# A two-layer sequence model in one launch: from four window stages in turn to five time blocks interleaved beside the experts

## What is computed

```
h = layernorm(x) * (1 + ca) + sa            # layer 0
q, k = l2norm(silu(conv4(silu(h W + b)))),  v = silu(conv4(silu(h Wv + bv)));  a, b = sigmoid(h Wa + ba), sigmoid(h Wb + bb)
S_t = a S - a b (S k) k^T + b v k^T;  o_t = q S_t          # 16 heads of 8x8, gated delta rule over 256 steps
x += ga * (o Wo + bo)
h = layernorm(x) * (1 + cb) + sb
x += gb * (h + sum over the top 2 of 8 experts of gate * (silu(h We1 + be1) We2 + be2))   # hidden size 512
h = layernorm(x) * (1 + ca') + sa'          # layer 1
x += ga' * out_proj(ssd(conv4(in_proj(h))))   # decaying state, normalised by its own weights
h = layernorm(x) * (1 + cb') + sb'
x += gb' * (down(gelu(up(h))))              # butterfly factors, folded once into two dense matrices
```

## Time and profile before

| | us |
|---|---|
| median of 3 runs | 811.51 |
| lowest and highest | 810.26, 816.49 |
| profiled execution, whole time | 816.03 |
| profiled execution, span of the core | 814.2 |

### The profile page before, as it was taken

The page is one execution under the profiler, slowest core; times in us unless marked ns, Lnnn a source line. Parts: engine busy times, 40 slices in busy tenths (PEclk is TensorE's granted clock), DMA queues, the critical chain, the costliest instruction groups (busy, mean ns, idle before and its releaser), DMA issues.

```text
span 814.2 us, 5816 instructions
## 1 busy us (share of the span) xinstructions
PE 503.1 (62%) x1910; PEld 285.1 (35%) x1910; DVE 379.4 (47%) x684; ACT 288.6 (35%) x397; POOL 249.8 (31%) x248
## 2 busy tenths in 40 slices
PE   6545146726639972537699826366898626999424
PEld 3113135312326630212377402123575212567101
DVE  1142489332647726666466366662665360012250
ACT  3343023244214344515244235233441523442222
POOL 1346323255511136347011262662112301100202
PEclk9976668755959995567899955579799756999656
DMA  9405450003320000130500000505000000000000
GB/s 322 175 0 116 105 180 14 0 0 93 88 52 1 1 0 0 43 72 14 116 1 1 0 0 3 114 0 130 0 1 1 0 0 0 14 1 1 0 0 13
DMA packets 9437, 34.08 MB, mean 42 GB/s; under 512 B 2488, under 2 KB 2496, under 8 KB 8128
## 3 DMA queue, kind: packets, MB, share of 16 engines
q1 hardware_dynamic: 9408, 33.71, 15.3%
HBM read 30.56 MB, written 3.15 MB: 41 GB/s over the span
## 4 chain that ended last, share of the span: by engine, by line
PE 37%; DVE 20%; ACT 7%; DMA 4%; issue 3%; POOL 2%; SPq 1%; POOLq 0%; DVEq 0%; ACTq 0%
PE psS L550 12%; PE psF L540 12%; DMA wrep<-scratch_dram 3%; PE psM L506 3%; DVE XK L982 2%; DVE work L952 2%; DVE work L980 2%; PE psB L441 2%; SPq L411 1%; PE psF L632 1%; PE psA L439 1%; PE psF L584 1%; DVE acc L991 1%; PE psS L497 1%; PE psF L578 1%
## 5 line engine op out<-in xcount | busy, mean ns | idle before, releaser
L540 PE MATMUL psF<-h,we1s 128*128 128x512 f32 x256 | 127.2, 630 | 39.4 <-ACT hid L807 38.6
L550 PEld LDWEIGHTS psS<-we2s,hid 128*128 128x128 f32 x1024 | 120.9, 195 | 15.1 <-issue 15.1
L807 ACT ACTIVATE hid<-psF,col 128x512 f32<-128x512 f32 x128 | 87.3, 686 | 97.5 <-PE psF L540 97.4
L550 PE MATMUL psS<-we2s,hid 128*128 128x128 f32 x1024 | 120.6, 277 | 0.0
L1296 POOL TENSOR_TENSOR work<-H,work 128x512 f32<-128x512 f32 x32 | 41.8, 1306 | 219.6 <-DVE H L1027 219.6
L991 DVE SCALAR_TENSOR_TENSOR acc<-psS,gate,acc 128x128 f32<-128x128 f32 x128 | 35.9, 343 | 103.8 <-PE psS L550 103.8
L540 PEld LDWEIGHTS psF<-h,we1s 128*128 128x128 f32 x256 | 42.7, 195 | 103.4 <-ACT hid L807 85.3
L441 PE MATMUL psB<-sq,C 128*128 128x512 f32 x32 | 29.8, 1031 | 47.2 <-ACT sq L700 47.2
L758 ACT ACTIVATE A<-ag 128x512 f32<-128x512 f32 x32 | 19.7, 626 | 98.9 <-DVE H L1027 98.9
L1010 DVE TENSOR_TENSOR pbuf<-wrep,H 128x512 f32<-128x512 f32 x32 | 22.5, 704 | 59.1 <-DMA wrep<-scratch_dram 58.8
L439 PE MATMUL psA<-x,C 128*128 128x512 f32 x32 | 27.0, 939 | 29.5 <-POOL x L1335 9.1
(11 more groups left out here) (191 smaller groups left out, 847.5 us busy)
## 6 DMA issues: line engine op xcount, KB each, us to landing
krep<-scratch_dram SPq DMA_DIRECT2D x32, 256.0 KB, 5.8
wrep<-scratch_dram SPq DMA_DIRECT2D x32, 256.0 KB, 5.9
hid<-fold_mats_dram SPq DMA_DIRECT2D x22, 256.0 KB, 8.1
we1s<-we_dram SPq DMA_DIRECT2D x1, 2048.0 KB, 12.3
we2s<-we_dram SPq DMA_DIRECT2D x1, 2048.0 KB, 16.7
x<-xT_dram SPq DMA_DIRECT2D x4, 256.0 KB, 6.8
scratch_dram<-work SPq DMA_DIRECT2D x4, 256.0 KB, 2.0
scratch_dram<-XK SPq DMA_DIRECT2D x4, 256.0 KB, 2.0
```

Source lines behind the costliest of these rows:

```text
L540: mm(psF[n % 2][:, :], we1s[:, e, k * P:(k + 1) * P], h2[:, :], start=True, stop=True).then_inc(s_hid_mm, 1)
L550: last = mm(psS[n % 2][:, t * P:(t + 1) * P], hid[n % 2][:, k, t * P:(t + 1) * P], we2s[:, e, k, :], start=(k == 0), stop=(k == HT - 1))
L807: nc.scalar.activation(hid[(EXPERTS * w + e) % 2][:, k, :], psF[n % 2][:, :], ACT.Silu, bias=pc("be1", HT * e + k)).then_inc(s_hid_done, 1)
```

## The change

The time axis is cut into five blocks of 32, 32, 64, 64 and 64 steps (`TWS`) instead of four of 64. SSD and FFN keep blocks of 64 (`BW`): block v is complete after the expert block given by `finished`. The loop becomes six rounds r. In round r each engine's queue is written out by expert e and quarter q: PE issues `first(r, e, q)` and a quarter of `second(r, e - 1, q)`, ACT `hidden(r, e, q)`, and between them stand, at fixed slots (e, q), the front of block r + 2 (LayerNorm, projections, convolution, norms, key products), the scan, attention output and router of block r + 1, and SSD and FFN of the block that round r - 1 finished. The last expert's `second` and last two mixes of a round fall into the next round. Front products use the banks X0, X1 (the two halves of `psM`) from block 2 on; router and attention output use `psB`.

Other parts: DVE solves for keys and values in one operation with two right sides (`solve`, in place of `solve_keys` and `solve_values`). LayerNorm scale and shift are eight activations per tile on ACT (`modulate`), one per sequence, instead of two tensor operations on POOL. The first convolution tap is computed by ACT (`first_taps`). `hidden` asks for Silu's table set before each tile. Query products and attention output work on halves of 32 steps. `h2`, `ag`, `gate` and `acc` get two buffers, `hf` holds one block and a carried column, `c3`/`KK`/`u` share `zb`. In the prologue only blocks 0 and 1 get a front; folding lies between their steps, and SP issues four of the later fold loads, then the spreads of block 0, then the other fold loads.

The other slots, as (e, q):
- PE: SSD center (2,0), variance (2,1), `ssd_in` (3,1), `ssd_out` (5,0); FFN center (5,3), variance (6,0), `ffn_up` (7,1) and (7,2), `ffn_down` (7,3); front center (2,2), variance (2,3), `project` (3,2) to (4,0), `square_sums` (5,2), `key_products` (6,2) to (7,0); `attn_out` (4,2) and (6,1); router's LayerNorm (7,0) and (7,1), `router` (7,3).
- ACT: `ln_square`, then one slot later `ln_scale` and `modulate`: SSD (2,0) (2,1), front (2,2) (2,3), FFN (5,3) (6,0), router (7,0) (7,1); `ssd_in` (3,1), `ssd_exp` (4,0), `ssd_norm` (4,3); `projected` (3,3) to (4,1), `first_taps` (4,1), `convolved` (5,2), `norms` (5,3); `attn_branch` (4,3) and (6,2); `ffn_act` (7,2), `ffn_out` and `routed` (7,3).
- DVE, by e, after that step's mix and chunks: `ssd_halo` 1, SSD LayerNorm 2, `ssd_decay` 3, `ssd_norm` 4, `ssd_branch` 5; front LayerNorm 2, `convolve` 5, `couple` 6 and 7; FFN LayerNorm 6; router's LayerNorm 7.

```diff
-WINDOWS = 4
-TW = SEQ // WINDOWS
+TWS = [32, 32, 64, 64, 64]
+W = len(TWS)
+T0 = [sum(TWS[:w]) for w in range(W + 1)]
+HALF = 32
+BW = 64
...
@@ PE @@
+            for r in range(W + 1):
+                vs = finished(r - 1) if r > 0 else []
+                v = vs[0] if vs else None
+                n, o = r + 2, r + 1
+                for e in range(EXPERTS):
+                    for q in range(4):
+                        if r < W:
+                            first(r, e, q)
+                        if e > 0 and r < W:
+                            second(r, e - 1, q)
+                        elif e == 0 and 0 < r:
+                            second(r - 1, EXPERTS - 1, q)
+                        if (e, q) == (0, 0) and r < W:
+                            logits(r)
+                        if (e, q) == (1, 0) and r < W:
+                            gate_rows(r)
+                        if (e, q) == (1, 1) and r < W:
+                            router_bias(r)
+                        if (e, q) == (1, 2) and r > 0:
+                            experts_back(r - 1)
...
 # in the same way: ssd center (2,0), variance (2,1), ssd_in (3,1), ssd_out (5,0), ffn center (5,3), variance (6,0),
 # ffn_up (7,1) (7,2), ffn_down (7,3); front center (2,2), variance (2,3), project (3,2) to (4,0), square_sums (5,2),
 # key_products (6,2) to (7,0); attn_out (4,2) and (6,1); moe center (7,0), variance (7,1), router (7,3)
@@ ACT @@
+            def modulate(key):
+                n = LN[key]
+                _, out, _, (s, c, l) = ln_tile(key)
+                act.wait_ge(s_ln_n1, n + 1)
...
+                for b in range(NB):
+                    last = nc.scalar.activation(out[:, b, :], out[:, b, :], ACT.Identity, bias=mod[:, 6 * l + s, b:b + 1],
+                                                scale=mod[:, 6 * l + c, b:b + 1])
+                last.then_inc(s_ln_h, 1)
-                nc.scalar.preload_act_table(ACT.Silu)
-                if w > 0:
-                    act.wait_ge(s_ffn_mm, w)
+            def hidden(w, e, k):
+                n = HT * (EXPERTS * w + e) + k
+                x_ = EXPERTS * w + e
+                c = ncols(w)
+                nc.scalar.preload_act_table(ACT.Silu)
+                act.wait_ge(s_hid_mm, n + 1)
+                if x_ > 1 and k == 0:
+                    act.wait_ge(s_eo_mm, x_ - 1)
+                nc.scalar.activation(hid[x_ % 2][:, k, 0:c], psF[n % 2][:, 0:c], ACT.Silu,
+                                     bias=pc("be1", HT * e + k)).then_inc(s_hid_done, 1)
...
+                        if r < W:
+                            hidden(r, e, q)
+                        if (e, q) == (0, 1) and r < W:
+                            route_exp(r)
+                        if o < W and q == 0 and 1 <= e <= 4:
+                            for i in range((e - 1) * nch // 4, e * nch // 4):
+                                decays(o, i)
+                        if (e, q) == (1, 0) and r < W:
+                            gate_rows(r)
...
 # then router_bias (1,1); ssd ln_square (2,0), ln_scale and modulate (2,1); the same for front (2,2) (2,3), ffn (5,3) (6,0),
 # moe (7,0) (7,1); ssd_in (3,1), ssd_exp (4,0), ssd_norm (4,3); projected (3,3) (4,0) (4,1), first_taps (4,1),
 # convolved (5,2), norms (5,3); attn_branch (4,3) and (6,2); ffn_act, all four, (7,2); ffn_out (7,3), routed (7,3)
@@ DVE @@
+            def solve(n):
...
+                X = work[:, 2:4, 0:ncols(n)].rearrange("p x (g i) -> p x g i", i=CH)
+                for j in range(CH - 1):
...
+                    v_.tensor_tensor(tmp, Gw(n, j)[:, :, 1:].unsqueeze(1).broadcast_to([P, 2, bc, k]),
+                                    X[:, :, :, j:j + 1].broadcast_to([P, 2, bc, k]), ALU.mult).then_inc(s_x_prod, 1)
+                    dve.wait_ge(s_x_prod, 7 * n + j + 1)
+                    v_.tensor_tensor(X[:, :, :, j + 1:], X[:, :, :, j + 1:], tmp, ALU.subtract).then_inc(s_x_sub, 1)
...
+                if r > 0:
+                    mix_expert(r - 1, EXPERTS - 2)
+                if r < W:
+                    route(r)
+                if r > 0:
+                    mix_expert(r - 1, EXPERTS - 1)
+                    experts_branch(r - 1)
+                if o < W:
+                    solve(o)
+                for e in range(1, EXPERTS):
+                    if r < W and e >= 2:
+                        mix_expert(r, e - 2)
+                    if e == 1 and n < W:
+                        carry_hf(n)
+                        carry(n)
+                    if e == 4 and v is not None:
+                        ssd_mix(v)
+                    if o < W and 1 <= e <= 4:
+                        for i in range((e - 1) * step, e * step):
+                            chunk(o, i)
...
 # then by e: ssd_halo 1, ln ssd 2, ssd_decay 3, ssd_norm 4, ssd_branch 5; ln front 2, convolve 5; ln ffn 6,
 # couple 0 and 1 in 6, 2 and 3 in 7; ln moe 7
@@ POOL @@
+                if r > 0:
+                    experts_residual(r - 1)
+                if o < W:
+                    hs = halves(o)
+                    for i in range(len(chunks(o))):
+                        read_state(o, i)
+                        if i == CPH + 1:
+                            attn_residual(hs[0])
+                if n < W:
+                    gates(n)
+                    decay_products(n)
+                if v is not None:
+                    ssd_residual(v)
+                if o < W:
+                    attn_residual(hs[-1])
+                if n < W:
+                    keys(n)
+                if v is not None:
+                    ffn_residual(v)
@@ SP @@
+            for j in range(RING, RING + 4):
+                fold_load(j)
             spread_keys(0)
             spread_solved(0)
-            for j in range(RING, len(FOLD_STEP)):
+            for j in range(RING + 4, len(FOLD_STEP)):
                 fold_load(j)
+            spread_keys(1)
+            spread_solved(1)
```

More of the change, by code:

```diff
@@ L48, with tokens_of_ln, ncols, chunks @@
 PACK = [(0, 6), (1, 5), (2, 4), (3,)]
+def tokens_of_ln(n):
+    return (0 if n == 0 else T0[n] + 1), min(T0[n + 1] + 1, SEQ)
+def ncols(w):
+    return NB * TWS[w]
+def chunks(w):
+    return range(T0[w] // CH, T0[w + 1] // CH)
+def halves(w):
+    return range(T0[w] // HALF, T0[w + 1] // HALF)
+def tiles(w):
+    return ncols(w) // P
+def mixed(w, e=0):
+    return EXPERTS * sum(tiles(i) for i in range(w)) + (e * tiles(w) if e else 0)
+def finished(w):
+    return [v for v in range(NV) if T0[w] < (v + 1) * BW <= T0[w + 1]]
+def last_window(v):
+    return [w for w in range(W) if v in finished(w)][0]
+def ln_order():
+    order = [("front", 0), ("front", 1), ("moe", 0)]
+    for m in range(W + 1):
+        v = [v for v in finished(m - 1)] if m > 0 else []
+        if v:
+            order.append(("ssd", v[0]))
+        if m + 2 < W:
+            order.append(("front", m + 2))
+        if v:
+            order.append(("ffn", v[0]))
+        if m + 1 < W:
+            order.append(("moe", m + 1))
+    return {key: i for i, key in enumerate(order)}
+LN = ln_order()
 def program(nc, xT, mats, consts, cols, cT, wmod, wo_rep, rw2, rb2, be2, we1, we2, lower, w_exp,
@@ new lines, in _ @@
+            for i in range(5):
+                project(0, i)
+            variance(("front", 1))
+            fold(0)
+            fold(1)
+            square_sums(0)
+            fold(2)
+            for g in range(4):
+                key_products(0, g)
+            for i in range(5):
+                project(1, i)
+            fold(3)
+            fold(4)
+            square_sums(1)
+            for i in range(5, STAGES):
+                fold(i)
+            attn_out(0)
+            center(("moe", 0))
@@ new lines, in _ @@
+            ln_scale(("front", 1))
+            modulate(("front", 1))
+            decays(0, 0)
+            decays(0, 1)
+            folded(4)
+            folded(5)
+            nc.scalar.preload_act_table(ACT.Silu)
+            for i in range(5):
+                projected(1, i)
+            first_taps(1)
+            for q in range(6, 10):
+                folded(q)
+            convolved(1)
+            norms(1)
+            decays(0, 2)
+            folded(10)
+            folded(11)
+            decays(0, 3)
@@ L1075, in ssd_halo, with experts_branch @@
+            def experts_branch(w):
+                k = ncols(w)
+                dve.wait_ge(s_yT_mm, w + 1)
+                if w > 0:
+                    dve.wait_ge(s_x2_done, w)
+                xs = sum(len(finished(i)) for i in range(w))
+                if xs > 0:
+                    dve.wait_ge(s_x4_done, xs)
+                v_.tensor_tensor(brS[:, 0:k], X0[:, 0:k], h2[w % 2][:, 0:k], ALU.add).then_inc(s_yf_done, 1)
             def ssd_halo(v):
@@ L1175, in _ @@
             v_.tensor_tensor(dbias[:, :], pc("bcon"), pc("downb"), ALU.add).then_inc(s_ub_done, 1)
-            carry(0)
+            carry_hf(1)
             convolve(0)
-            couple(0)
-            solve_keys(0)
```

(9 more changed lines are left out.)

1564 lines of the change are left out of this document (847 added, 717 removed).

## The result

| | us |
|---|---|
| after, median of 4 runs | 890.87 |
| lowest and highest | 889.86, 891.62 |
| before, median beside it | 813.44 |
| ratio to before, with 95% interval | 1.0962 [1.0932, 1.0992] |
| forecast | 851 (735 to 905) |

The account below looks back on a forecast made before the run. No engine is full; a chain through five in-order queues bounds the kernel. Prologue 102, rounds 110, 139, 184, 150, 92 and tail 65 give 842; PE's clock adds 12, 1.8 around makes 856, lowered to 851 us (735 to 905; own range 805 to 900).

Parts of the forecast that it names:

- (c): Round 2, after solve: DMA round trip of the solved keys, 14.4 us.
- (d): Round 2, after the DMA: scan chunk 0 at 4.2 us and chunk 1 beside POOL at 5.2, 9.4 us.
- (e): Round 2: a mix, two chunks and the SSD LayerNorm's product, with ACT waiting in modulate, 11 us.
- (k): Round 2, its end: last LayerNorm 7, Gelu with its load 5, three slots and router 7, 19 us.
- (a): Round 2, its start: five slots, router exponential, two decays and gate rows, the transpose and experts_branch, 16 us.
- (f): Round 2: DVE waits for ACT's modulate, slots, LayerNorm steps and a decay, then the scan, 16 us.
- (g): Round 2: a chunk, ssd_decay, mix and ssd_mix, two chunks and norm, 32 us.
- (i): Round 2: Silu, Square, sums, a slot and norms with two loads 13 us; FFN LayerNorm among three slots 12.
- (j): Round 2: POOL's residual, four products and seven key products, then PE, center and Square, 17 us.
- rival 2: Redundant table loads are dropped, so slots on the chain lose 1.28 us until PE binds: 788 us, chance 0.07.
- The overlap works: Decays at slot (2,0) find their chunk done, so rounds cost only ACT's busy time: 655 us, chance 0.17.
- PE takes ACT's place: PE stays at its lower clock, its slot of 3.6 us passing ACT's 1.97: 940 us, chance 0.10.

Follow-up runs that it names:

- experiment 8: Changed kernel with one activation of 512 columns for the eight of a LayerNorm's scale and shift, using the first sequence's values for all: 857.0 us, ratio 1.0550.
- e137_all_three: Changed kernel with table loads only where the set changes, solve early, and the scan a step later with LayerNorm products ahead of it: 781.9 us, ratio 0.9639.
- experiment 11: Changed kernel with useless matmuls on PE ahead of square_sums and the first key_products of rounds 0 to 2: 887.93 us, ratio 1.0904.

## Why the prediction came out too short, though its mechanism held

**The mechanism held.** The end is set by a chain that winds through five in-order queues, not by a full engine. Its two obstacles were the ones named: the loads (49 us for all 144 that need not be there) and the scan that isn't ready at slot (2,0) (39 us by either edit). With both mended and the LayerNorm products ahead, the kernel is faster than before. Of the pieces of round 2, those on DVE from `solve` on were forecast within 0.5 us each: (b) `solve` 11.0 for 11.5, (c) the round trip 14.2 for 14.4, (d) 9.4 for 9.4, (e) 11.1 for 11. The prologue took 104 for 102 and the tail 64 for 65.

**The step that failed is the sum of the rounds, by its small terms.** It gave 675 us and the rounds took 721, so the slowdown came out twice as large as forecast. The 12 us set aside for PE's clock belong to the 46 that are missing, so for 34 the sum had nothing. Three terms were mis-sized: piece (k) at 19 us, which took 24.9, since ACT waits there for products of the FFN on PE that I had left out; `modulate` at 2.0 us a LayerNorm, which took 2.76; and the convolution at 8.9 us, which took 10.9 in round 2. They come to about 25 of the 46.

*Modulate* was put at 0.25 us an instruction, near the end of tiny tiles. The trace has 427 ns for one of 64 columns and 2.76 us for eight in a row. Thirteen of them are on the chain between the first and the last round, 33.6 us where 26 were counted: 8 of the 46. My bound let half of it lie in waits; by experiment 8 nearly all of it is on the path. The Trainium skill, "ScalarE: Activation LUTs", section "What ACT_TABLE_LOAD costs", gives 186 ns plus 0.833 for each column, 93 more for each pointer operand, and an overlap of 93 in a row. That makes an estimate of 425 ns alone and 332 in a row; the trace agrees with the first, and has 345 for the second. By that estimate the term would have been 2.7.

*Piece (k)* took 24.9 for 19. All engines, from 537 to 561 us:

```profile
537.24 1.88 PE L748 MATMUL psM<-hS,wx 128*128 128x512 f32 x4
...
542.12 2.76 ACT L896 ACTIVATE h<-h,mod 128x64 f32<-128x64 f32 x8 [0.76 <-DVE h L1219]
...
546.90 1.28 ACT L1065 ACT_TABLE_LOAD   x1
548.19 1.26 ACT L1073 ACTIVATE zb<-psM,ubias 128x512 f32<-128x512 f32 x2
549.03 3.75 PE L748 MATMUL psM<-hS,wx 128*128 128x512 f32 x4 [7.29 <-ACT zb L1073]
551.11 0.69 ACT L1073 ACTIVATE zb<-psM,ubias 128x512 f32<-128x512 f32 x1 [1.65 <-PE psM L748]
...
552.57 1.61 PE L699 MATMUL psF<-h,we1s 128*128 128x512 f32 x2
...
552.82 0.69 ACT L1073 ACTIVATE zb<-psM,ubias 128x512 f32<-128x512 f32 x1 [1.02 <-PE psM L748]
...
554.90 3.60 PE L755 MATMUL psM<-zb,wc 128*128 128x512 f32 x8
...
558.54 0.69 ACT L1082 ACTIVATE brS<-psM,dbias 128x512 f32<-128x512 f32 x1 [3.04 <-PE psM L755]
```

I counted the Gelu with its load, three slots and the router, and left out that the second half of `ffn_up` and `ffn_down` stand on PE between them: 3.75 and 3.60 us here, partly where I had slots. ACT waits for them 1.65, 1.02 and 3.04 us, 5.7 in all, which is nearly the whole of what (k) lacked. The same three waits are 6.0 us in round 3 and 3.4 in round 4, so 15 of the 46 lie here. Also, L748 takes 0.94 us a matmul after 7.3 us of standing, at a granted clock of 0.50. At 537.24, where PE had worked on, it takes 0.47 (1.88 for four) at 1.00: the two levels of its clock, 1.2 and 2.4 GHz.

*The convolution* on DVE took 10.9 us for 8.9 in round 2, with POOL's decay products beside it. I took the mean of four windows of the kernel before, where the single windows range from 7.82 to 9.71.

The rest of round 2 is spread: (a) took 18 us for 16, (f) and (g) together 51 for 48, and (i) and (j) together 48 for 42. I did not settle these one by one, so some 20 of the 46, PE's clock among them, stay open. Of (a), part is `experts_branch` waiting 12.2 us for PE.

A further 5 us come from the last step. The forecast was lowered by 0.55% because the profiled execution of the kernel before lay that far above its median; that of the changed kernel, 891.07, lay on its own.

Three sums of the prediction don't come out as written. (a) to (k) add up to 183, not 184. The upper bounds, with half of `modulate`'s, reach 967 and not the 900 of the own range, for which no reason is given. And 61 us off 851 is 790, not the 788 of rival 2.

**The rivals.** *The overlap works* was not the case as built: at slot (2,0) the wait was there. Its place was right: in e137_all_three, where ACT no longer waits before the first of these copies, the kernel takes 781.9 and is faster than before, but that is with the loads gone too, and far from 655. ACT's busy time is no floor that the rounds come near. *Redundant loads are dropped* is excluded by 160 loads of 1283 ns; without them the kernel took 842, not 788. Of these 54 us only 12 are the loads' (49 less where I had 61); the rest is what the forecast itself lacked. *PE takes ACT's place* is not seen: the granted clock was 0.74 to 0.92 in the rounds, and the measured time is 49 us short of this rival's 940. What PE's lower level costs in the rounds was not measured by itself (experiment 11).

**Where the 77 us are.** The loads account for 49, `solve` behind the branch and the scan a step too early for 39 each, `modulate` for 34. These overlap and don't add: loads with the early solve gave 77, and with the later scan as well 109. Against the costs stand some gains, of which the fused solve (3) and POOL's relief (9) were measured in the kernel before. I had priced the second at nothing but its activations. What the narrower first two blocks and `first_taps` are worth was not tried.

## What to carry to other kernels

Before interleaving stages by hand on in-order queues, walk each queue past the first instruction that can wait for another engine, and count what stands behind it. Here a few lines in another order were worth 39 us, nearly as much as the 49 of 144 table loads. A table load that the code asks for costs its 1.28 us also when the set is in place: ask for it where the set changes. And price an engine's relief from both sides: what it gives up, and whom it stops disturbing.

## What the hardware showed that I had not expected

POOL and DVE disturb each other more than I had priced: with two POOL operations fewer in each LayerNorm, nine taps of the convolution went from 1057 to 939 ns each on average, and the decay products on POOL from 965 to 837. Eight activations of 64 columns take 2.76 us, against 0.81 for the one of 512 that e2_one_modulate has in their place. And of 189 us of ACT work taken away, 49 came back, while of 35 us in `modulate` 34 did: the busy time of a line says little of its worth; its place in the chain says most.
